# State-space layers rewritten around one scan over both channel tiles, and layer norms moved at five seams

## The reference: sixteen layers over four batches

```python
xi, z = split(x @ in_proj)                      # 256 channels each
u = silu(conv1d(xi, 4 taps, causal) + conv_b)
dtr, Bc, Cc = split(u @ x_proj)                 # 64, 16 and 16 columns
delta = softplus(dtr @ dt_proj + dt_b)          # 256 channels
h = exp(delta[:, :, None] * A) * h + (delta * u)[:, :, None] * Bc   # per token, in order
y = einsum('bdn,bn->bd', h, Cc)
out = ((y + u * D) * silu(z)) @ out_proj
```

## Time and profile before

| | us |
|---|---|
| median of 3 runs | 2807.47 (2795.40 to 2813.47) |
| the profiled execution | 2810.36 (its span: 2808.6) |
| PE busy | 2359.8 (84%) |
| DVE busy | 1763.0 (63%) |
| ACT busy | 1270.4 (45%) |
| POOL busy | 645.0 (23%) |
| scans of layer 10, first start to last batch's end | 279.07 |
| the same in layer 14 | 277.89 |

### The profile page before, as it was taken

How to read it: one execution, slowest core, us unless ns; L and a number is a source line. 1 busy time by engine, 2 the same in 40 slices (tenths; PEclk the granted TensorE clock), 3 DMA queues, 4 the chain that set the end, 5 groups by cost and what they waited for, 6 DMA issues and landing times. The chain is left out here.

```text
span 2808.6 us, 30635 instructions
## 1 busy us (share of the span) xinstructions
PE 2359.8 (84%) x9720; PEld 1010.9 (36%) x9760; DVE 1763.0 (63%) x2747; ACT 1270.4 (45%) x2497; POOL 645.0 (23%) x740
## 2 busy tenths in 40 slices
PE   8999999767389889779987699777779989877878
PEld 3333334312122244454553244222224447322323
...
DMA packets 9358, 25.92 MB, mean 9 GB/s; under 512 B 1072, under 2 KB 7280, under 8 KB 8176
## 3 DMA queue, kind: packets, MB, share of 16 engines
...
## 5 line engine op out<-in xcount | busy, mean ns | idle before, releaser
L3222 PE MATMUL l_py<-l_read,w_const 128*128 128x512 f32 x512 | 316.0, 703 | 93.2 <-DVE l_read L3355 74.8
L3499 POOL TENSOR_TENSOR l_drive<-l_du,l_bsb 128x512 f32<-128x512 f32 x256 | 326.1, 1296 | 208.0 <-ACT l_bsb L3296 187.9
L3346 DVE TENSOR_TENSOR_SCAN l_state<-l_decay,l_drive 128x512 f32<-128x512 f32 x256 | 310.2, 1212 | 60.8 <-ACT l_decay L3304 53.2
L398 ACT ACTIVATE l_probs<-l_psp,l_stats 128x512 f32<-128x512 f32 x256 | 172.9, 682 | 150.5 <-DVE l_stats L408 150.5
L3304 ACT ACTIVATE l_decay<-l_delta,l_a 128x512 f32<-128x512 f32 x256 | 176.4, 690 | 138.6 <-DVE l_state L3346 138.3
L259 POOL TENSOR_TENSOR l_nx_small<-l_nx_small,w_const 128x4 f32<-128x4 f32 x36 | 36.7, 1019 | 776.5 <-DVE l_nx_small L253 776.5
L3222 PEld LDWEIGHTS l_py<-l_read,w_const 128*128 128x128 f32 x512 | 98.4, 213 | 247.1 <-DVE l_read L3355 208.5
L1268 DVE TENSOR_REDUCE l_tops<-l_ring 128x2 f32<-128x1024 f32 x128 | 151.5, 1220 | 45.6 <-PE l_ring L1259 45.3
L406 DVE TENSOR_REDUCE l_stats<-l_psp 128x2 f32<-128x1024 f32 x128 | 156.1, 1220 | 35.9 <-PE l_psp L360 35.1
L3355 DVE TENSOR_TENSOR l_read<-l_state,l_pc 128x512 f32<-128x512 f32 x256 | 168.0, 656 | 0.0
L714 DVE SCALAR_TENSOR_TENSOR l_product<-l_psu,w_gated,l_first 128x512 f32<-128x512 f32 x104 | 78.0, 750 | 137.5 <-ACT l_first L688 137.4
...
## 6 DMA issues: line engine op xcount, KB each, us to landing
...
```

The costliest lines, as they stand in the source:

```text
L398: act.activation(probs[:, s % 4, i, :], psp[:, s % 2, i, :], ACT.Exp, bias=stats[:, s % 4, 1, i:i + 1], scale=scale, accum_out=stats[:, s ...
L3222: pe.matmul(py[:, t, :], eye, read[:, s % 4, :], start=n == 0, stop=n == NS - 1, skip_group_check=True)\
L3346: dve.tensor_tensor_scan(state[:, s % 4, :], decay[:, s % 2, :], drive[:, s % 4, :], 0.0, ALU.mult, ALU.add).then_inc(L["state"].sem, 1)
L3499: pool.tensor_tensor(drive[:, s % 4, :], du[:, b % 2, t, :], bsb[:, n % 2, :], ALU.mult)\
```

## The change

1. **State-space layers.** One scan works over both channel tiles, 1024 elements a partition, so 64 scans in a layer instead of 128. `decay` moves from PSUM to SBUF, in a ring of three such pairs; its first column in each tile is set to zero once, which makes the scan start anew at the second tile. `drive` has a ring of three, made by one POOL product a pair; `state` and `read` have two pairs. The skip term is two products by a diagonal matrix on PE at a batch's start, instead of two DVE operations. For all batches but the first, the positive part of the softplus is an ACT Relu. Silu reads PSUM directly. `u` and `du` are no longer double. PE issues both add_ups one behind the other and spreads B four states ahead. z is projected before x.
2. **Norms.** Layers 2, 10 and 14 now hold `nx`, and layers 2, 10 and 15 hold `late`; the blocks n3, n11 and n15 are gone. In layer 2 the three `nx` norms stand at the end of its slots, from x = 130, each eight slots behind the one ahead.
3. **Layer 8.** `ask_above` stands directly behind `ask_below`, and `divide` ahead of `nx.eps`; `nx.diag` moves to the next round, behind its first scans; on PE `nx.centre` stands ahead of `add_below`.

The diff, cut to its core:

```diff
-                    if is_batch(a):
-                        add_below(pe, a)
                     if normed(o):
                         nx.centre(pe, o)
                     if is_batch(a):
+                        add_below(pe, a)
                         add_above(pe, a)
...
+                    if normed(o - 1):
+                        nx.diag(dve, o - 1)
+                    if is_batch(a):
...
+                        ask_above(dve, a)
                     if normed(o):
                         nx.keep(dve, o)
                     if is_batch(a):
-                        ask_above(dve, a)
+                        divide(dve, a)
                     if normed(o):
                         nx.eps(dve, o)
-                    if is_batch(a):
-                        divide(dve, a)
-                    if normed(o):
-                        nx.diag(dve, o)
...
-def state_space(nc, core, name, g):
+def state_space(nc, core, name, g, inner, last_in):
+    PAIRS = B * NS
+    RING = 3
...
-        drive, state, read = (L.sb(n, [P, 4, S]) for n in ("drive", "state", "read"))
+        decay, drive = (L.sb(n, [P, RING, CT, S]) for n in ("decay", "drive"))
+        state, read = (L.sb(n, [P, 2, CT, S]) for n in ("state", "read"))
-        decay, pc, py = (L.ps(n, [P, 2, S]) for n in ("decay", "pc", "py"))
-        pb, front = L.ps("pb", [P, S]), L.ps("front", [P, S])
+        positive = y
+        front, pc, py = (L.ps(n, [P, 2, S]) for n in ("front", "pc", "py"))
+        pb, out = L.ps("pb", [P, S]), L.ps("out", [P, S])
+        kept, square = L.sb("kept", [P, 1, S]), L.sb("square", [P, S])
+        nx = NextNorm(L, out[:, :], buffers=(kept, square, square[:, :].rearrange("p (t q) -> p t q", q=P)))
+        late = NextNorm(L, out[:, :], last=True, shared=nx)
...
+        def add_skip(pe, b, t):
+
+            if b:
+                pe.wait_ge(L["gated"].sem, L["gated"].at(b - 1, t + 1))
+            else:
+                pe.wait_ge(L["skip_diag"].sem, L["skip_diag"].at(0, t + 1))
+            pe.matmul(py[:, t, :], skip_diag[:, t, :], u[:, t, :], start=True, stop=False, skip_group_check=True)
+
+        def add_up(pe, k):
+            pe.wait_ge(L["read"].sem, L["read"].at(0, k + 1))
+            for t in range(CT):
+                mm = pe.matmul(py[:, t, :], eye, read[:, k % 2, t, :], start=False, stop=k % NS == NS - 1,
+                               skip_group_check=True)
+            mm.then_inc(L["summed"].sem, 1)
...
             if b + 1 < B:
-                if n < 4:
-                    project_x(pe, b + 1, n // 2, (0, 1) if n % 2 == 0 else (2, 3))
-                if n == 6:
+                if n < 2:
+                    project_z(pe, b + 1, n)
+                if 2 <= n < 6:
+                    project_x(pe, b + 1, (n - 2) // 2, (0, 1) if n % 2 == 0 else (2, 3))
+                if n == 7:
                     project_low(pe, b + 1)
-                if n in (7, 9):
-                    project_delta(pe, b + 1, (n - 7) // 2)
-            if n in (11, 12):
-                project_z(pe, b, n - 11)
-            if n == 13 and b:
-                project_out(pe, b - 1)
+                if n == 9:
+                    project_delta(pe, b + 1)
+            if b:
+                if n == 1:
+                    project_out(pe, b - 1)
+                if n == 5:
+                    nx.centre(pe, b - 1)
+                if n == 8:
+                    nx.var(pe, b - 1)
+                if n == 12:
+                    nx.spread(pe, b - 1)
...
-            s = b * ST + n * CT + t
+        def decays(act, k, t):
+
+            b, n = divmod(k, NS)
             if n == 0:
                 act.wait_ge(L["delta"].sem, L["delta"].at(b, t + 1))
-            if s >= 2:
-                act.wait_ge(L["state"].sem, L["state"].at(0, s - 1))
-            act.activation(decay[:, s % 2, :], delta[:, b % 2, t, :], ACT.Exp, scale=a[:, t, n:n + 1])\
+            if k >= RING:
+                act.wait_ge(L["state"].sem, L["state"].at(0, k - RING + 1))
+            act.activation(decay[:, k % RING, t, 1:], delta[:, b % 2, t, 1:], ACT.Exp, scale=a[:, t, n:n + 1])\
...
-        def scan(dve, s):
-            dve.wait_ge(L["decay"].sem, L["decay"].at(0, s + 1))
-            dve.wait_ge(L["drive"].sem, L["drive"].at(0, s + 1))
-            if s >= 4:
-                dve.wait_ge(L["read"].sem, L["read"].at(0, s - 3))
-            dve.tensor_tensor_scan(state[:, s % 4, :], decay[:, s % 2, :], drive[:, s % 4, :], 0.0,
+        def scan(dve, k):
+
+            dve.wait_ge(L["decay"].sem, L["decay"].at(0, CT * (k + 1)))
+            dve.wait_ge(L["drive"].sem, L["drive"].at(0, k + 1))
+            if k >= 2:
+                dve.wait_ge(L["read"].sem, L["read"].at(0, k - 1))
+            dve.tensor_tensor_scan(state[:, k % 2, :, :].rearrange("p t s -> p (t s)"),
+                                   decay[:, k % RING, :, :].rearrange("p t s -> p (t s)"),
+                                   drive[:, k % RING, :, :].rearrange("p t s -> p (t s)"), 0.0,
                                    ALU.mult, ALU.add).then_inc(L["state"].sem, 1)
...
-                dve.scalar_tensor_tensor(out=y[:, t, :], in0=u[:, b % 2, t, :], scalar=w("skip", t, t + 1),
-                                         in1=py[:, t, :], op0=ALU.mult, op1=ALU.add).then_inc(L["skip"].sem, 1)
...
-                dve.tensor_tensor(y[:, t, :], y[:, t, :], zs[:, b % 2, t, :], ALU.mult).then_inc(L["gated"].sem, 1)
+                dve.tensor_tensor(y[:, t, :], py[:, t, :], zs[:, b % 2, t, :], ALU.mult).then_inc(L["gated"].sem, 1)
...
+                    add_up(pe, k)
+                    if k + 4 < PAIRS:
+                        spread_b(pe, k + 4)
+                    if k + 2 < PAIRS:
+                        spread_c(pe, k + 2)
+                    between(pe, b, n)
...
-                        if n == 5:
+                    decays(act, k, 0)
+                    if k + 1 < PAIRS:
+                        copy_b(act, k + 1)
+                    if b and n == 7:
+                        nx.square(act, b - 1)
+                    if ahead:
+                        if n in (4, 5):
+                            raw_z(act, b + 1, n - 4)
+                        if n == 8:
                             for t in range(CT):
-                                if ahead:
-                                    silu_x(act, b + 1, t)
+                                silu_x(act, b + 1, t)
                             for t in range(CT):
-                                if b:
-                                    silu_z(act, b - 1, t)
-                        if n == 8 and ahead:
+                                silu_z(act, b + 1, t)
+                        if n == 9:
                             copy_low(act, b + 1)
-                        if n in (9, 11) and ahead:
-                            magnitude(act, b + 1, (n - 9) // 2)
-                        if n == 11 and ahead:
-                            soft_exp(act, b + 1)
-                        if n == 12 and ahead:
-                            soft_log(act, b + 1)
-                        if n in (13, 14):
-                            raw_z(act, b, n - 13)
-                for t in range(CT):
-                    silu_z(act, B - 1, t)
+                        if n == 11:
+                            for t in range(CT):
+                                magnitude(act, b + 1, t)
+                                positive_part(act, b + 1, t)
+                            for t in range(CT):
+                                soft_exp(act, b + 1, t)
+                        if n == 12:
+                            for t in range(CT):
+                                soft_log(act, b + 1, t)
...
+                    scan(dve, k)
+                    if k:
+                        read_out(dve, k - 1)
+                    if b:
+                        if n == 1:
                             gate(dve, b - 1)
+                        if n == 4:
                             finish(dve, b - 1)
-                read_out(dve, B * ST - 1)
-                add_skip(dve, B - 1)
+                        if n == 8:
+                            nx.keep(dve, b - 1)
+                        if n == 10:
+                            nx.eps(dve, b - 1)
...
...
+                    pool.tensor_tensor(drive[:, k % RING, :, :], du[:, :, :],
+                                       bsb[:, k % 2, :].unsqueeze(1).to_broadcast([P, CT, S]), ALU.mult)\
+                        .then_inc(L["drive"].sem, 1)
...
-NORMALISES_NEXT = (0, 1, 3, 4, 5, 6, 7, 8, 9, 11, 12)
-NORMALISES_LAST = (1, 3, 4, 5, 6, 7, 8, 9, 11, 12, 13)
+NORMALISES_NEXT = (0, 1, 2, 3, 4, 5, 6, 7, 8, 9, 10, 11, 12, 14)
+NORMALISES_LAST = (1, 2, 3, 4, 5, 6, 7, 8, 9, 10, 11, 12, 13, 15)
```

447 lines of the change are left out of this document (250 added, 197 removed).

## The result

The changed kernel takes 2951.22 us (median of 4 runs, 2945.87 to 2954.46), the kernel before 2801.43 beside it: ratio 1.052, 95% interval 1.049 to 1.055. It is slower, as forecast, but by 150 us instead of 52 to 58 (2859 less 2807.47 or less 2801.43), and outside the range of 2788 to 2912.

The account below looks back on a forecast made before the run. State-space stages were taken as bound by DVE, afterwards by scan and drive excluding each other. Layers +110, late norm +3.5, seams -42, layer 8 -20: +51 on 2810.4, 2862, as a median 2859; range 2788 to 2912.

Parts of the forecast that it names:

- The exclusion: State-space layers: a scan with two SBUF inputs and POOL's drive cannot run together; chance 0.68, own range 2815 to 2905.
- the first rival: State-space layers: scans and POOL's drives do not exclude each other; 3.45 us a pair, 2791 us, chance 0.20.
- 4.4 us a pair: Scans: scan and drive hold each other off, 2.1 + 2.3 us a pair, with 4.2 and 4.7 as ends.
- The stalls behind ACT, and the split: Middle batch: 10.3 us of scans waiting behind ACT, less 3 of side work fitting in; DVE's split 2.3.
- The table excursion (pair 8): ACT at n=8: 4.8 us, and 1.9 for decay, copy, decay, less the pair's 4.4; entered as +1.5.
- the delta: At n=11, ACT's magnitudes, positive parts and exponentials wait for PE's delta, had 3 us into the scan: +4.5 us.
- 328 us of scans a layer: State-space layer: four batches of 81, 85, 85 and 77 us against 279.07 before, +49 a layer.
- A pair on DVE alone: DVE: scan of 1024 and its read take 3.3 us a pair against 3.42, gaining at most 7 us a layer.
- The half clock: PE in the scans: half clock behind pauses costs 2 us a batch, +6 a layer, 0 and 20 as ends.
- The seams: Layer boundaries: norms moved into the layers save 42 us in sum, between -24 and -58.
- layer 8: Batches with a norm fall from 23.68 to 17 us, -6.7 in three batches, -20 (ends -8 and -25).
- the give-backs: Seam gains partly returned inside layers, such as 10 us for layer 2's three norms and 4 for `late`.

Follow-up runs that it names:

- drive_after_scan: The changed kernel with POOL's drive of the next pair also waiting for this pair's scan to end: 2894.91 us, ratio 1.032 to the kernel before.
- slots_first: The changed kernel with PE issuing the spread of B, then the side products, and add_up last in each pair: 2828.08 us, ratio 1.008 to the kernel before.

## Why the prediction was right or wrong

- **The exclusion** was right in kind, and it is what gave the forecast its sign: from three meetings of other operations in the trace to a scan. Taken away in two ways, 114 and 139 us go; put alone into the kernel before, it costs 94. The trace of before had a row for the scan as well (L2396 above), which the prediction missed; the first rival's chance of 0.20 was given without it. The rival named 2791, not slower than before. With the scan out of the exclusion the pairs do come at 3.6, but the kernel takes 2837, 34 us more than before. So the sign would have been the same without the exclusion, for a reason that the prediction did not have, and in that part it was luck. The sum's own price of the exclusion, 2859 less 2791, is 68 us; with the early order it measures 70, with the order that was forecast 114.
- **4.4 us a pair** was the first term that failed. Where both engines simply take turns the pairs come at 3.9 to 4.3, at the lower end of 4.2 to 4.7 or below it. But I let the turns be free. The drive of the next pair comes first, since ACT's copy stands ahead of the second decay, and then it sits in the loop of scan, read, add_up, spread and copy, which I had priced without it (6.9 for two pairs). The first seven pairs of the second batch are 5.07 on the mean, and all eleven without a long stall 4.99 (0 to 6, 10, 12, 14 and 15): 0.6 too little, 6 to 7 us a batch. `drive_after_scan` shows that the order counts, but its steady 4.88 takes back only 1.3 of these.
- **The stalls behind ACT, and the split**, 10.3 less 3 and 2.3 in a middle batch, were the second term that failed. Over pairs 7 to 13 the batch takes 53.2 us, where the sum has some 45. Pair by pair the rows have 7.28, 6.74, 11.82, 3.54, 10.35, 5.59 and 7.86; the terms of the sum, each laid on its pair, give 6.3, 5.9, 6.7, 4.4, 8.9, 5.8 and 7.6. The table excursion (pair 8) is thus near, and by its own two terms, 4.8 + 1.9, it would have been right. The largest miss is pair 9. DVE has no idle time there: a scan held by a drive, its read, and a split of 6.86 us, priced at 2.3, of which the casts of 2.47 and 2.55 are 5.0. So this miss is the exclusion's, not ACT's. A cast beside a drive was already in the trace of before (L3322, 1.37 in the median and 0.42 alone). That two drives came just then fits ACT's copy of low, which waited 4.2 us for its product, at nothing in the sum, and the copy of B stood behind it. For the delta I took PE's product as done 3 us into the scan of n = 11. The row has an add_up at half clock ahead of it, behind a scan that was itself late, and a wait of 12 us. Each stall was priced from a full-speed start, and none handed its lateness on. `slots_first` shows the cause of what is not the exclusion: 84 us hang on side products that stand behind an add_up, and 39 on the spread of B that stands there too.
- 328 us of scans a layer in the sum, 378.6 in the trace: +49 forecast (55 with the clock), +99.6 measured (the layer itself +102.0): about twice.
- **A pair on DVE alone** at 3.3 us was a little low: without exclusion and stalls it is 3.53 to 3.60, more than the 3.42 of two single tiles before. The rows have the 0.2 us: before, a scan starts 0.07 ahead of the end of the read in front of it (1875.66), in the changed kernel 0.13 behind it (1891.77, 1891.90). In the code the scan now waits for just that read, since `state` has two pairs; that this wait is the reason is not tested. The pair scan would not have paid on DVE even alone.
- **The half clock** at 2 us a batch: 2.8 in the one batch that was tried. It is the right size for what added work restored; the whole of it was not measured.
- **The seams** (-42, measured -42.3) and **layer 8** (-20, measured -21.9) were right one by one within 2 us, closer than two traces of the same code agree, and the give-backs inside layer 2 (444.1 to 456.2) and layer 3 (118.1 to 122.6) too.
- Most signs named ahead of the result were seen: scan rows above 2.3, drives up to 4.3, ACT's square behind PE's centre (5.9 us), batches of layer 8 under 17. The steady stretch of pairs every 4.3 to 4.5 us was not: 4.30 stands between 3.9 and 6.2. "Over 360 for layer 10" was named as what would make it wrong, and it is 379.

The Trainium skill's rule in SBUF — State Buffer, section on the two separate sides, is borne out for the scan, with 3.06 against 2.29 us for its row beside a drive. (What the prediction calls a product and a copy are an addition, L3338, and a product, L3448.)
